# Ten copies of idle rows ahead of the late loads, one read of each late word on VectorE, and second products one turn sooner from the fifth end tile

## The reference

```
x = x + gnn(layernorm(x), adj)      # 32 graphs of 256 nodes, hidden width 512, RMS norm, SiLU
xn = layernorm(layernorm(x)) * gamma + beta
logits = xn @ Wr + br               # 8 experts
top_vals, top_idx = top_k(logits, 2);  w = softmax(top_vals)
y = sum over the two chosen e of  w_e * (gelu(xn @ W1[e] + b1[e]) @ W2[e] + b2[e])   # 128 -> 256 -> 128
x = x + y
```

## Time and profile before

| | before |
|---|---|
| median of 3 runs | 411.95 us |
| the profiled execution | 411.64 us |
| its span in the trace | 409.9 us |
| PE busy | 382.9 us, 93% |
| POOL busy | 314.2 us, 77% |
| DVE busy | 301.2 us, 73% |
| ACT busy | 277.7 us, 68% |
| mean granted TensorE clock | 0.995 |

### The profile page before, as it was taken

The page is one execution under the profiler, slowest core; times in us unless marked ns, Lnnn a source line. Parts: engine busy times, 40 slices in busy tenths (PEclk is TensorE's granted clock), DMA queues, the critical chain, the costliest instruction groups (busy, mean ns, idle before and its releaser), DMA issues. The chain is left out here.

```text
span 409.9 us, 11327 instructions
## 1 busy us (share of the span) xinstructions
PE 382.9 (93%) x2598; PEld 326.3 (80%) x2598; DVE 301.2 (73%) x1290; ACT 277.7 (68%) x653; POOL 314.2 (77%) x440
## 2 busy tenths in 40 slices
PE   1899999999999999999789996999999999999994
PEld 1467777767777777777569996999999899999993
DVE  5687789999999999998865752566666666765562
ACT  1377777787778898779878554677777776555540
POOL 1223378877787899888888879997787677999984
PEclk9999999999999999999999999899999999999999
DMA  7879974444423442221266355555555544331111
GB/s 227 259 242 337 338 232 137 141 144 142 139 88 115 156 144 79 76 69 55 68 157 180 111 156 140 158 150 153 145 153 156 156 124 110 108 87 40 38 38 38
DMA packets 43472, 57.25 MB, mean 140 GB/s; under 512 B 6224, under 2 KB 36176, under 8 KB 42768
## 3 DMA queue, kind: packets, MB, share of 16 engines
q1 hardware_dynamic: 35200, 36.74, 32.4%
q0 software_dynamic: 6096, 18.52, 12.9%
q10 hardware_dynamic: 2112, 1.27, 1.1%
HBM read 41.80 MB, written 22.31 MB: 156 GB/s over the span
## 5 line engine op out<-in xcount | busy, mean ns | idle before, releaser
L572 POOL DMA_INDIRECT out<-result,rows_in x92 | 90.3, 981 | 27.8 <-DVE result L1573 15.8
L822 PE MATMUL banks<-w_sb,hidden_e 128*128 (+1 forms) x736 | 102.7, 281 | 2.8 <-DVE result L1573 2.4
L822 PEld LDWEIGHTS banks<-w_sb,hidden_e 128*128 128x128 f32 x736 | 92.2, 193 | 4.7 <-issue 4.2
L962 ACT ACTIVATE hidden_e<-banks 128x512 f32<-128x512 f32 x92 | 54.9, 597 | 45.4 <-PE banks L805 43.6
L515 POOL DMA_INDIRECT rows_dram<-rows_out,row_of x64 | 65.3, 1021 | 13.4 <-issue 10.6
L649 PE MATMUL banks<-gw_sb,agg 128*128 128x512 f32 x128 | 65.2, 595 | 0.9 <-DVE gw_sb L1013 0.9
L673 PE MATMUL banks<-hidden_t,gw_sb 128*128 128x256 f32 x256 | 62.3, 386 | 1.7 <-ACT hidden_t L885 1.7
L528 POOL MEMSET space<- 128x620 f32 x100 | 63.0, 630 | 0.1
L673 PEld LDWEIGHTS banks<-hidden_t,gw_sb 128*128 128x128 f32 x256 | 46.4, 190 | 16.1 <-ACT hidden_t L885 7.3
L1108 DVE TENSOR_TENSOR hidden<-banks,rms_bc 128x512 f32<-128x512 f32 x64 | 43.8, 685 | 15.3 <-ACT hidden L870 15.1
L955 ACT ACTIVATE xg_t<-banks,ones 128x128 f32<-128x128 f32 x92 | 33.3, 362 | 22.0 <-PE banks L785 21.9
(11 more groups left out here) (148 smaller groups left out, 741.2 us busy)
## 6 DMA issues: line engine op xcount, KB each, us to landing
rows_in<-rows_dram SPq DMA_DIRECT2D x92, 132.5 KB, 2.3
adj<-adj_t SPq DMA_DIRECT2D x16, 512.0 KB, 5.0
x_tok<-x SPq DMA_DIRECT2D x16, 256.0 KB, 6.1
x_d<-x_t SPq DMA_DIRECT2D x16, 256.0 KB, 4.8
rows_dram<-idle_in POOLq DMA_DIRECT2D x1, 3710.0 KB, 13.9
rows_dram<-idle_in SPq DMA_DIRECT2D x28, 132.5 KB
out<-result,rows_in POOLq DMA_INDIRECT x92
w_sb<-w SPq DMA_DIRECT2D x1, 1024.0 KB, 8.3
```

The costliest lines, as they stand in the source:

```text
L572: nc.gpsimd.indirect_dma_start(out=out, out_offset=bass.IndirectOffsetOnAxis(ap=rows_in[:, i % RING][:, IDX_AT:IDX_AT + 1].bitcast(U32), a ...
L822: last = pe.matmul(y_ps(i)[:, w], hidden_e[:, i % 4, w * HCE + c], w2_sb[:, bass.ds(at + c * D, D)], start=(c == 0 and i >= EARLY), stop=( ...
L962: nc.scalar.activation(hidden_e[:, i % 4], h_ps(i), ACT.Gelu).then_inc(gelu_done, 1)
```

## The change

Three edits:

1. SP issues 10 of the 28 idle copies before the late loads instead of 14 (`AT_ONCE`); the other 18 follow one behind every second late load, the last one behind load 55 instead of load 47. All still land before the first end tile is loaded.
2. DVE no longer reads the word of a late tile a second time. For tiles from 20 on, low and sum take their register values from `words`, where base and high have left them.
3. PE makes the second product of a tile in step i + 3 instead of i + 4 from tile 69 on, the fifth of the end tiles (`CLOSER` is 68). Step 72 holds the second products of tiles 68 and 69; the last step, 95, is gone.

```diff
+AT_ONCE = 10
...
+        CLOSER = NT + 4
...
             sp.wait_ge(ends_ready, 1)
-            for c in range(NC // 2):
+            for c in range(AT_ONCE):
                 fill_end(c)
...
             for i in range(EARLY, NT):
                 load_rows(i)
-                if i % 2 and i - EARLY < NC:
-                    fill_end(NC // 2 + (i - EARLY) // 2)
+                if i % 2 and (c := AT_ONCE + (i - EARLY) // 2) < NC:
+                    fill_end(c)
...
+            def second_products(step):
+
+                i = step - NARROW_LAG
+                tiles = [i] if i < CLOSER else [i, i + 1] if i == CLOSER else [i + 1]
+                return [i for i in tiles if 0 <= i < TILES]
...
-                if (i := tile_at(step, NARROW_LAG)) is not None:
+                for i in second_products(step):
                     if i < NT and i % PER_WORD == 0:
...
                     last.then_inc(y_done, 1)
+                if step >= NARROW_LAG:
                     tail(step, 2)
...
-            for step in range(TILES + NARROW_LAG):
+            for step in range(TILES + NARROW_LAG - 1):
...
-                    if j < NT and j % PER_WORD == 0:
-                        done_words[j // PER_WORD % 2] = dve.value_load(word[0:1, j // PER_WORD:j // PER_WORD + 1],
-                                                                       min_val=0, max_val=2 ** 24 - 1)
+                    if j < EARLY and j % PER_WORD == 0:
+                        words[j // PER_WORD % 2] = dve.value_load(word[0:1, j // PER_WORD:j // PER_WORD + 1],
+                                                                  min_val=0, max_val=2 ** 24 - 1)
...
-                                                   done[:, bass.ds(expert(done_words, j, 1, True) + W_AT, 1)],
+                                                   done[:, bass.ds(expert(words, j, 1, True) + W_AT, 1)],
...
-                                                   done[:, bass.ds(expert(done_words, j, 1, False) + W_AT, 1)],
+                                                   done[:, bass.ds(expert(words, j, 1, False) + W_AT, 1)],
```

1 line of the change is left out of this document (removed).

## The result

| | before | changed |
|---|---|---|
| median (lowest to highest), same chip | 412.21 us (411.73 to 412.53, 6 runs) | 405.41 us (404.88 to 406.13, 6 runs) |
| ratio, 95% interval | | 0.984 [0.9824, 0.9856] |
| the profiled execution | 411.64 us | 404.88 us |
| its span | 409.9 us | 403.1 us |
| mean granted TensorE clock | 0.995 | 0.993 |

Faster by 6.8 us, where 9.9 were forecast: 402.1 us in a range of 400.3 to 405.0, and the measured median lies 0.4 us above it. The changed trace follows, in the views of before. Busy time by engine: turns 24 to 39, 39 to 64, 64 to 91, and a stretch at a low clock. Columns: stretch, us, then PE, PEld, DVE, ACT, POOL, clock, DMA share, GB/s.

A forecast was written before the change was run, and what follows sets the result against it. PE was taken as the bound, losing time to late load 20 and DVE's word reads. 5.54 + 4.95 + 0.4 - 1.1 = 9.8 us off 411.64 gave 401.8, as a median 402.1 us, range 400.3 to 405.0.

The forecast's parts named there:

- copies: Before turn 20: four fewer idle copies bring load 20 forward, so turn 24 comes 5.54 us sooner; bounds 0 to 5.6.
- words: Turns 39 to 64: without DVE's second word read PE should not wait at all, 4.95 us gained; at least 2.5.
- second products: Kernel's end: fewer second products after the last first product let POOL's last send start sooner, 0.4 us; bounds 0 to 0.5.
- POOL: Late sends: stretched by DVE's base adds, they keep DVE's pace at 4.14 us lag, costing 1.1 us; bounds 0 to 7.0.
- What bounds the kernel: PE at its 1.896 us floor in late steps, except turn 20 waiting for load 20 and DVE's pace costing 4.95 us.
- a large term fails: Rival: load 20 held by something else or DVE still pacing PE in turns 39 to 64; 404.6 to 407.6 us; chance 0.09.
- POOL becomes the bound: Rival: POOL's sends tied to DVE for half of the tiles or more; 404.5 to 408 us; chance 0.11.
- the stall forecast for the last GELU: At PE's end: only tile 90's second product covers tile 91's GELU, so the last product stalls 0.1 us.
- The Trainium skill's inference: Case at POOL's sends: DVE's adds from SBUF hold no send, so the sum is 1.1 us lower, 401.0; chance 0.19.
- The issue cost of a copy: SP's queue before load 20: an idle copy costs 1.31 to 1.39 us to issue, against the skill's rule giving 2 to 4 in all.
- The loads falling behind: Rival, until load 55: load pairs with a copy between take longer than PE's 3.79 us, so PE idles; 413 us; chance 0.02.
- The median: Whole kernel: the runs' median lies 0.3 us above the profiled execution, so 401.8 becomes 402.1 us.

The follow-up runs named there:

- again_late: The changed kernel run once more unaltered, on chip D: 399.55 us, ratio 0.972 to the kernel before.
- two_reads: The changed kernel with DVE's second read of late words put back, and separate registers for low and sum: 410.74 us, ratio 0.9923 to the kernel before.
- lag4: The changed kernel with second products of end tiles in step i + 4 again: 405.37 us, ratio 0.9818 to the kernel before.
- columns15: The changed kernel with PE's column transposes in step 15 instead of 14 and DVE's word table a step later: 404.60 us, ratio 0.9772 to the kernel before.
- plain_again: The changed kernel with every result sent to fixed rows by a plain transfer, second run, on chip E: 399.89 us, ratio 0.9708 to the kernel before.

## Why the prediction was wrong, point by point

Compared from turn 0 on, so that the first half of the program stays out (before 56.11 to turn 24, 197.60 to the last send):

| term | predicted | result's trace | again_late (no held signal) |
|---|---|---|---|
| copies: turn 24 sooner | 5.54 | 2.17 (53.94) | 6.09 (50.02) |
| words: turns 24 to 64 shorter | 4.95 | 4.96 (75.83) | 4.95 (75.84) |
| second products and POOL: from turn 64 to the last send | 0.4 - 1.1 = -0.7 | -0.90 | +0.38 |
| sum | 9.8 | 6.23 | 11.42 |

- **What bounds the kernel, and the words: right.** Both views of it, turns 39 to 64 at the floor and DVE waiting for PE, came as said. Only the 0.05 us a tile by which DVE was still to fall behind did not come: low 60 starts 0.37 us behind its last matmul, so the register instructions of low and sum were worth something too. Under two_reads the loss was 6.6 us instead of 4.95. There DVE reaches turn 24 late already (low 24 is 3.8 us behind its product, 2.3 before); how much of that is the sooner turn 24 and how much a held signal was not told apart.
- **The copies: this step failed**, by 3.37 of 5.54 us. That load 20 comes sooner and that turn 20 no longer waits for it was right: SP took from 232.19 to 246.68, 1.45 us a copy instead of 1.39. What failed was the sentence "Turn 24 then comes at 250.38 + 4 x 2.12", which took turn 19 as fixed. Turn 19 had 3.66 us of slack behind it, and where PE's signals are held, steps 9 to 16 are longer by about as much: in the changed kernel turn 16 comes 9.30 us behind turn 14 instead of 5.74, and nothing behind it takes that up any more. For the same reason "and with it the low clock, which came only behind that idle time" failed: the idle time came back in step 14, and the low clock with it. The one trace of before had no held signal of this size, so no row of it could say this; its second trace has it, hidden. Where nothing is held the term is 6.09, and the step is right. As a bound the prediction gave "0 (something else holds load 20)". The time lies where "a large term fails" (0.09) and "POOL becomes the bound" (0.11) have it, and came by neither mechanism: load 20 was held by nothing, and no row of sends was tied from tile 20 on. Nor would the time have been right without held signals: 11.45 us off, on chip D, is more than the 9.9 forecast, and 399.55 is below the range.
- **The second products: not settled by themselves.** lag4 gives 1.2 us with intervals that overlap. PE's last two products took 2.07 us in one piece, 0.1 more than 16 rows do, which is the stall forecast for the last GELU.
- **POOL: the tie came, its cost of 1.1 us is not shown.** Eleven sends were tied, 4.13 us behind their own sums where 4.14 had been worked out. But two things lay otherwise. Send 5 started at 246.88 and not near 243.99, which the prediction held to be touched by no edit: the held signals had made POOL late as well. And the last send waited for the last sum, late by a held signal; 1.26 us behind send 90 it could have started at 398.45, not at 399.13, so POOL did not set the end. That this term and the one before it come to -0.90 where -0.7 was forecast is therefore luck. Where nothing was held (again_late) a tie formed a step nearer, 2.24 us behind the sums, and cost nothing, since the last send stood 1.1 us behind the last sum. The Trainium skill's inference ("SBUF — State Buffer", section "Who interferes with whom"), by which such an add leaves the sends alone, is not borne out for these sends: they took 1.10 instead of 0.96 us where they began 0.08 us behind a base. All traces together say when: a send that begins 0.10 to 0.22 us behind a base ends 1.18 to 1.19 us behind the base's start, one that begins 0.03 to 0.06 behind it takes its 0.96 and the add some 0.36 to 0.38 instead of 0.35, and between, at 0.07 to 0.09, most are stretched. Whether what meets is the reading of the row numbers or the making of the descriptors, no run tells apart.
- **The issue cost of a copy** stood against the Trainium skill's rule that the time to start a DMA is usually small relative to the DMA itself ("DMA: Bandwidth & Descriptors", section "Issuing engines are not separate DMA queues"). By the rule the term was estimated at 2 to 4 us, and the result's 2.17 seems to say so. The rows say otherwise: SP needed 1.45 us a copy, and the term is 6.09 where no signal is held.
- **The loads falling behind: did not happen.** No turn waited for a load in any trace of the changed kernel.
- **The median**: 405.4 lies 0.5 above the profiled execution, so the result is not that of one bad execution. The changed kernel took 404.15 and 404.80 us on chips A and E and 399.55 on D; on B and C it did not run unaltered, and columns15 on B took 404.60.

## What to carry to other kernels

A wait on the critical path also swallows disturbances before it, and with it go the low clock and whatever else follows from the wait. When an edit takes the wait away, expect to pay for what it swallowed, and look for that in a second trace of the kernel before, step by step, not in the sum. If single runs of a kernel scatter by 1% on some chips and hardly on others, look for consumers on two engines that are released at the same moment long after their product: here that was one cause, not two. Leaving out a spacer behind scatters with indices (a MEMSET that nobody reads) cost 4.6 us here, so try it before you cut such a tile as idle work.

## What the runs showed of the hardware

- Signals of TensorE reach ACT and DVE 1.5 to 4 us late at times, and POOL about 1 us, on four chips of five (and the one of the result). With plain transfers in place of the results' scatters with indices no trace shows one, and the kernel takes 399.15 and 399.89 us instead of some 404.5. Without space between the scatters it takes 409.21 instead of 404.60 on one chip, with six held signals between tiles 46 and 70; with half the space, on another chip, the trace shows four. Scatters of rows 1.6 to 1.8 us apart hold nothing by themselves (plain_again).
- A plain transfer of a result holds POOL for 0.54 us, a scatter for 0.96.
- A scatter of results that begins 0.08 us behind one of DVE's adds from SBUF takes 1.10 us, one that begins 0.15 behind it 1.03, and a row of them then keeps DVE's pace of 1.90 us for some ten sends, at a lag behind their own sums of 2.2, 4.1, 8.0 or 9.8 us. With 700 columns of scratch this put the end of the kernel 3 us behind POOL's floor.
- Neither space nor order shortened the run of six last sends: the scatters stood 1.25 to 1.27 us apart in every kernel in which results were waiting.
